# Taking a reciprocal root from GpSimd to ScalarE and VectorE, and splitting an exponential block

## The reference

```python
xn = _layernorm(x)
q, k, v = xn @ Wq.T + bq, xn @ Wk.T + bk, xn @ Wv.T + bv   # 16 heads, 4 key/value heads, width 32
q, k = _rope(_rmsnorm(q, qn_w)), _rope(_rmsnorm(k, kn_w))
# local attention: each token sees itself and 64 tokens before it
local = softmax(where(mask, -10000, q @ k.T * scale)) @ v @ Wo.T + bo
# routed attention: one key and value head is chosen for each token
gating = softmax(xn @ W_gate.T); head = argmax(gating)
k_shared, v_shared = fk[head], fv[head] * max(gating)
routed = causal_softmax(q2 @ k_shared.T / sqrt(32)) @ v_shared
return x + local + routed
```

## Time and profile before

| what | us |
|---|---|
| runs | 684.29, 685.91, 686.01 |
| median | 685.91 |
| span of the profiled execution, first to last instruction | 684.4 |
| TensorE busy | 646.0 |
| VectorE busy | 496.3 |
| GpSimd busy | 442.6 |
| ScalarE busy | 362.5 |

### The profile page before, as it was taken

How to read it: one execution, slowest core, us unless ns; L and a number is a source line. 1 busy time by engine, 2 the same in 40 slices (tenths; PEclk the granted TensorE clock), 3 DMA queues, 4 the chain that set the end, 5 groups by cost and what they waited for, 6 DMA issues and landing times.

```text
span 684.4 us, 19451 instructions
## 1 busy us (share of the span) xinstructions
PE 646.0 (94%) x7432; PEld 510.2 (75%) x7432; DVE 496.3 (73%) x1328; ACT 362.5 (53%) x906; POOL 442.6 (65%) x368
## 2 busy tenths in 40 slices
PE   3788999999999899999899899999999999999997
PEld 3577888887788688888688667777777777777775
DVE  3956966677678866787676368888888787879454
ACT  4436444472527344445335555556566566656674
POOL 3965764938195735684487267685868777778730
PEclk9979999999999999999999999999999999999999
DMA  8522213231232032222214541321314131402011
GB/s 295 206 59 86 82 38 115 86 98 51 66 102 61 30 112 70 64 70 74 77 32 118 158 142 56 96 64 50 111 49 110 51 106 32 110 28 87 4 33 33
DMA packets 64942, 56.61 MB, mean 83 GB/s; under 512 B 6481, under 2 KB 48849, under 8 KB 64849
## 3 DMA queue, kind: packets, MB, share of 16 engines
q1 hardware_dynamic: 62704, 54.45, 27.2%
q10 hardware_dynamic: 2144, 0.93, 0.5%
HBM read 37.20 MB, written 17.89 MB: 80 GB/s over the span
## 4 chain that ended last, share of the span: by engine, by line
PE 78%; DVE 9%; POOL 4%; ACT 3%; issue 2%; DMA 2%; ACTq 1%; DVEq 0%; POOLq 0%
PE gemm L938 17%; PE s_ps L1047 12%; PE od_ps L1096 11%; PE st_ps L1080 10%; PE gemm L1024 6%; PE od_ps L1110 5%; PE win L998 3%; PE gemm L934 3%; PE win L983 2%; PE s_ps L1119 2%; DMA rope_t<-rope 2%; PE av L1010 2%; DVE l_sum L1266 2%; ACT p_loc L1492 2%; DVE l_max L1257 1%
## 5 line engine op out<-in xcount | busy, mean ns | idle before, releaser
L938 PE MATMUL gemm<-w_tok,xt 128*128 128x512 f32 (+1 forms) x768 | 186.1, 384 | 3.3 <-DVE x_res L1283 0.9
L938 PEld LDWEIGHTS gemm<-w_tok,xt 128*128 128x128 f32 x768 | 131.7, 193 | 28.2 <-issue 1.4
L1318 DVE CUSTOM_DVE_ANT_0 s_ps<-s_ps,x_ln 128x512 f32<-128x512 f32 (+3 forms) x224 | 127.6, 620 | 24.4 <-PE s_ps L1047 24.0
L1047 PE MATMUL s_ps<-k_stack,w_tok 96*128 96x512 f32 (+2 forms) x336 | 101.5, 385 | 0.3 <-DVE x_res L1283 0.3
L1080 PE MATMUL st_ps<-w_tok,k_stack 98*128 98x512 f32 x288 | 99.0, 413 | 0.2 <-ACT p_loc L1540 0.2
L1540 ACT ACTIVATE p_loc<-st_ps 128x512 f32<-128x512 f32 x144 | 77.7, 599 | 36.0 <-PE st_ps L1080 34.8
L1634 POOL TENSOR_TENSOR rope_b<-qkv,sin_t 128x128 f32<-128x128 f32 (+1 forms) x32 | 27.5, 880 | 79.5 <-DVE qkv L1232 79.3
L1047 PEld LDWEIGHTS s_ps<-k_stack,w_tok 96*128 96x128 f32 x336 | 55.0, 188 | 28.3 <-DVE picked_fk L1318 12.4
L1492 ACT ACTIVATE p_loc<-win,l_max 128x96 f32<-128x96 f32 x256 | 60.9, 391 | 19.1 <-DVE l_max L1257 19.0
L934 PE MATMUL gemm<-xt,w_qt 128*128 128x256 f32 x384 | 57.1, 293 | 6.3 <-DVE picked_fv L1211 3.5
L1540 ACT ACTIVATE p_loc_t<-st_ps 128x512 f32<-128x512 f32 x96 | 52.4, 599 | 19.8 <-PE st_ps L1080 19.3
(11 more groups left out here) (172 smaller groups left out, 1298.7 us busy)
## 6 DMA issues: line engine op xcount, KB each, us to landing
w_tok<-q_parts SPq DMA_DIRECT2D x72, 128.0 KB, 2.6
q_parts<-qt SPq DMA_DIRECT2D x120, 64.0 KB
x_ln<-x SPq DMA_DIRECT2D x8, 512.0 KB, 4.7
x_res<-x SPq DMA_DIRECT2D x16, 256.0 KB, 2.9
partial<-x_res SPq DMA_DIRECT2D x16, 256.0 KB, 2.6
w_tok<-partial SPq DMA_DIRECT2D x8, 512.0 KB, 5.2
raw<-w_tok SPq DMA_DIRECT2D x3, 1024.0 KB, 12.9
v_win<-v_rows SPq DMA_DIRECT2D x64, 48.0 KB, 2.2
```

The costliest lines, as they stand in the source:

```text
L938: i = e.matmul(g[:, 0:cols], xs[l][:, k, a * P:(a + 1) * P], w_tok_p[r][:, k, c0:c0 + cols], start=first, stop=last)
L1047: e.matmul(s_ps[bank][:, 0:cols], q_op[b][0:HALVES, i, h, :], k_stack[0:HALVES, b * S + c0:b * S + c0 + cols], start=True, stop=True).then ...
L1318: e.tensor_tensor_reduce(out=s[:, 0:cols], in0=s[:, 0:cols], in1=causal[:, S - width + c0:S - width + c0 + cols], scale=1.0, scalar=dst if ...
```

## The change

The power on GpSimd (step 2 above) goes. In its place, ScalarE takes the logarithm of `rms_v` and the exponential of -1/2 times it, into `rms_e` (plan step `q_root`), and VectorE makes one Newton step of three instructions, y = e (1.5 - 0.5 e e v), into `rms_y` (plan step `q_newton`). The table set that holds both functions is loaded once, before the first exponential. Mean + eps is now formed from a tensor of eps, by another kind of instruction. The 16 exponentials of a local tile, one step of the plan before, are four steps of four, between which the plan can put other work of ScalarE. The last two chunks of qt wait in the plan for the last tile's norm, and in `first_maxima` the order of two small steps around a `yield` changes.

```diff
@@ take_q @@
         do("q_rms", n, a)
+        yield 0, [("V", 1.3)]
+        do("q_root", n, a)
+        yield 0, [("A", 0.5)]
+        do("q_newton", n, a)
+        yield 0, [("V", 0.6)]
         do("q_rope", n, a)
-        yield 0, [("V", 1.1), ("G", 3.6), ("G", 1.6), ("", SLACK)]
+        yield 0, [("G", 1.4), ("", SLACK)]
+        p.roped = (n, a) == LAST_TILE
         yield from attend(n, a)

     def take_qt(n, kind, c, freed):
+        while (n, c) in LAST_CHUNKS and not p.roped:
+            yield None
@@ attend @@
-        do("weights", m, a)
-        def exps_end(end):
-            win_free[:] = [end - 1.1 * (HKV - 1 - g) + HOP for g in range(HKV)]
-        yield 0, [("A", 4.4)], exps_end
+        for g in range(HKV):
+            do("weights", m, a, g)
+            yield 0, [("A", 1.1)], lambda end, g=g: win_free.__setitem__(g, end + HOP)
@@ first_maxima @@
         do("max_in_rows", 0, 0)
-        yield 0.11, [("A", 0.27)]
         do("max_low", 0, 0)
-        yield 0, [("V", 0.35)]
+        yield 0.11, [("A", 0.27), ("V", 0.35)]
@@ vector_program @@
-                e.tensor_scalar(rms_v[:, :], rms_t[:, :], 1.0 / DK, RMS_EPS, ALU.mult, ALU.add).then_inc(
-                    *M["rms_v_r"].did((n, a)))
+                e.scalar_tensor_tensor(rms_v[:, :], rms_t[:, :], 1.0 / DK, rms_eps[:, :].to_broadcast([P, NH]),
+                                       ALU.mult, ALU.add).then_inc(*M["rms_v_r"].did((n, a)))
+
+            elif step == "q_newton":
+                n, a = key
+                lane.wait_ge(*M["rms_e"].of((n, a)))
+                e.scalar_tensor_tensor(rms_t[:, :], rms_e[:, :], -0.5, rms_e[:, :], ALU.mult, ALU.mult).then_inc(
+                    *seq.did())
+                lane.wait_ge(*seq.now())
+                e.tensor_tensor(rms_t[:, :], rms_t[:, :], rms_v[:, :], ALU.mult).then_inc(*seq.did())
+                lane.wait_ge(*seq.now())
                 if n or a:
-                    lane.wait_ge(*M["rms_r"].of(tile_before(n, a)))
+                    lane.wait_ge(*M["rope_r"].of(tile_before(n, a)))
+                e.scalar_tensor_tensor(rms_y[:, :], rms_t[:, :], 1.5, rms_e[:, :], ALU.add, ALU.mult).then_inc(
+                    *M["rms_r"].did((n, a)))
@@ scalar_program @@
+        e.preload_act_table_set("natural_log_exp_and_others")
         e.activation(warm[:, :], minus_half[:, :], ACT.Exp).then_inc(*M["warmed"].did())
+            elif step == "q_root":
+                n, a = key
+                lane.wait_ge(*M["rms_v_r"].of((n, a)))
+                if n or a:
+                    lane.wait_ge(*M["rms_r"].of(tile_before(n, a)))
+                e.activation(rms_e[:, :], rms_v[:, :], ACT.Ln).then_inc(*M["rms_l"].did((n, a)))
+                lane.wait_ge(*M["rms_l"].of((n, a)))
+                e.activation(rms_e[:, :], rms_e[:, :], ACT.Exp, scale=-0.5).then_inc(*M["rms_e"].did((n, a)))
@@ gpsimd_program @@
-            elif step == "q_rms":
-                n, a = key
-                lane.wait_ge(*M["rms_v_r"].of((n, a)))
-                if n or a:
-                    lane.wait_ge(*M["rope_r"].of(tile_before(n, a)))
-                e.tensor_tensor(rms_y[:, :], rms_v[:, :], minus_half[:, :].to_broadcast([P, NH]), ALU.pow).then_inc(
-                    *M["rms_r"].did((n, a)))
```

26 lines of the change are left out of this document (15 added, 11 removed).

## The result

The changed kernel takes 726.5 us (725.4 to 726.6) against 686.0 us of the kernel before: a ratio of 1.0588, 95% interval 1.0564 to 1.0612. The forecast was 683.1 us, with 691 us as its upper end. It is wrong in sign and by 43 us. One further execution, in which TensorE's matmuls took longer throughout, took 1122.1 us and is left out.

A forecast was written before the change was run, and what follows sets the result against it. TensorE was taken as nearly full, with 32.8 us not busy in the first stage to win. Terms -1.1 - 1.9 + 1.2 - 1.0 = -2.8 us gave 683.1 us from 685.91; range 678 to 691 for 8 in 10.

The forecast's parts named there:

- Term 1: First tile: norm slightly earlier, three products fill TensorE's wait before the transposes; -1.1 us (bounds 0 and -1.15).
- Term 2: Around 52 to 56 us: exponentials in four steps let a copy and a bank-freeing pick come sooner; -1.9 us (-0.5 to -2.0).
- Term 3: Middle of first stage: 18 us of VectorE stalls cost TensorE 5.8 us, less 4.6 us regained; +1.2 us (-6 to +14).
- against it stands what the same reshuffle gives back: Between 180 and 340 us, 4.6 us of TensorE's 8.1 us hole could close, as exponentials no longer block ScalarE.
- Term 4: End of first stage: last tile's scores start 2.1 us sooner, scaled weights hang on later exponentials; -1.0 us (-3 to +2).
- The power frees VectorE of nothing: Across tiles: GpSimd's power does not hold VectorE up, so removing it gives VectorE 0 us.
- the Newton step stalls VectorE: Rival, middle: Newton instructions wait behind GpSimd's 2.76 us scaling, with a bank's read behind them; 691.7 us, chance 0.21.
- The reshuffle wins more: Rival: earlier norms and split exponentials shrink the 8.1 us hole of 180 to 340 us to 2; 678.1 us, chance 0.15.
- full TensorE hides it all: Rival: the 3.0 us won before 60 us are lost again in the new order's other holes; 685.9 us, chance 0.29.
- No table was reloaded: Judges the rival that logarithm and exponential need other tables, two loads per tile on ScalarE; above 700 us, chance 0.01.
- The routed stage is the same: After the first stage: every engine's list is the same in both kernels from the routed stage's two first scores on.
- What would show it: Forecast's list of profile signs for right or wrong, such as over 3 us idle between 60 and 180 us if wrong.

The follow-up runs named there:

- after_newton_first: Changed kernel with VectorE's Newton step moved ahead of the sum l_sum and its reciprocal in six tiles, other engines' order kept; 715.0 us, ratio 1.0420.
- after_order_exp: Changed kernel without the Newton step, ScalarE's exponential writing rms_y itself, order otherwise the same; 706.5 us, ratio 1.0284.
- after_order_pow: Changed kernel's order, with GpSimd's power in place of the logarithm, exponential and Newton step; 706.7 us, ratio 1.0300.
- The nudges: Kernel before with one assumed planner time changed, same instructions: power 3.6 to 3.4 us, 689.0 us; exponentials 4.4 to 4.2 us, 699.9 us.
- pow_early_block: Changed kernel with GpSimd's power for the new arithmetic and exponentials planned as one block, the plan still assuming an early norm; 734.8 us, ratio 1.0720.

## Why the prediction was wrong, point by point

- **Term 1 (-1.1 us, the first tile): not there.** The transposes no longer wait, as forecast, and rms_y is ready at 37.0 us (forecast 37.3). But the wait did not go, it moved to the three products put ahead of them. Changed kernel, timeline of 37 to 40 us, VectorE and TensorE:

```profile
36.82 0.18 DVE L1263 SCALAR_TENSOR_TENSOR rms_y<-rms_t,rms_e 128x20 f32<-128x20 f32 x1
36.91 0.16 DVE L1192 TENSOR_REDUCE g_rank<-g_score 128x1 f32<-128x16 f32 x1
37.11 1.32 DVE L1194 TENSOR_SCALAR g_hot<-g_score,g_rank 128x16 f32<-128x16 f32 x1
38.35 0.41 DVE L1270 TENSOR_TENSOR qt<-gemm,qt 128x256 fp32r<-128x256 f32 x1
```

```profile
38.82 1.65 PE L944 MATMUL gemm<-w_tok,xt 128*128 128x512 f32 x3 [1.03 <-DVE qt L1270]
```

  The step "TensorE, free from 39.01 - 1.15 = 37.86, is busy with them until 38.7" failed: these products need the bank that qt L1270 frees, and g_hot ahead of it stood 1.32 us behind GpSimd's multiplication (1.26 us from 37.14), which the earlier norm puts there. I had asked when the norm is ready, not when the bank of what fills the hole is free.
- **Term 2 (-1.9 us, the exponentials): half.** The stretch of 52 to 56 us is busy for 3.34 us against 2.01, 1.3 us better. Over the first 60 us the idle time is the same to 0.1 us, so no lead came out of terms 1 and 2.
- **Term 3 (+1.2 us, the middle): this is the step that failed.** Its first half was right: VectorE's stall behind the scaling, forecast as 18 us, measured in the three Newton groups as 10.2 + 7.0 + 5.9 less 16 x (0.178 + 0.115 + 0.178) = 15.6 us. Six tiles, not four, had it behind the scaling. Its price was wrong, in four ways. First, "0.32 us for each us" had been read from the order of before, where the stalls stood beside other work (and it divides the waits of 200 to 340 us by the stalls of 60 to 340). The Newton step puts its stall ahead of bank reads: 19.1 us of time for 15.6 of stall. Of that, the waits are 55.8 - 43.9 = 11.9 us and TensorE's longer busy time is 384.1 - 376.0 = 8.1 us. Second, "against it stands what the same reshuffle gives back", 4.6 us, had the wrong sign: the order alone costs 20.7 us, 11.3 of waits and 9.2 of busy time (from the table: 43.9 - 32.6, 376.0 - 366.8). This part keeps the new form of rms_v, too. Third, the three instructions themselves, 11 us of VectorE in the forecast, had been priced at nothing because VectorE and ScalarE "have more idle than that in the first stage". after_newton_first, where they never stall, is still 8.5 us above after_order_exp, so the 19.1 us are not all the price of stalls. Fourth, the bound of +14 "if TensorE loses 1 us for each" was no bound, since a wait can take the clock with it: 23.2 us of waits brought 17.3 of slower matmuls.
- **Term 4 (-1.0 us, the end of the stage): wrong in sign, small.** In the last 20.8 us TensorE is busy for 15.7, so it stands still for 5.1 us against 4.1, at a clock of 0.84.
- **The power frees VectorE of nothing: right.** after_order_pow and after_order_exp agree within 0.2 us, with intervals of 1.3 and 2.1 us to either side, and VectorE's busy time does not fall without the power. In the profile of before, fk_stack ran seven times within a power, in 0.17 to 0.20 us each. By the rule of the Trainium skill that the prediction weighed (SBUF — State Buffer, Who interferes with whom), it should have been held up.
- **The rival "the Newton step stalls VectorE" had the mechanism and the sign**, with a chance of 0.21 and a price of 691.7 us. It had no term for the clock and none for a worse order. "The reshuffle wins more" was refuted, and so was "full TensorE hides it all". No table was reloaded: the trace has one load, of 1.28 us, at the start.
- **The routed stage is the same: right** (284.1 and 284.2 us).
- "What would show it" named the signs that came: idle time of more than 3 us between 60 and 180 us (8.7), waits on bank reads behind the Newton lines, ScalarE waiting before the logarithm (18.1 us in 7 waits).

Still open: the 14.8 us that the new order costs with the short scaling. The nudges show that orders this close differ by up to 14 us, and pow_early_block that the early norm is worse than that by itself; which of its placements does it was not isolated. The new form of rms_v is in these 14.8 us, too.

## What to carry to other kernels

Where one engine is full and others feed it in order, do not price a new instruction by its own length alone, or by what stalls cost elsewhere in the trace. Ask what stands behind it in its queue, and what long GpSimd instruction can run beside it; cutting that one into four was worth 22 us in the changed kernel and 3 us in the one before. A planned order is part of the kernel: cross order and arithmetic in separate kernels before judging either, and nudge one planner number to see how far an order alone moves the time. Waits of TensorE can be paid twice, when its clock falls behind them, so a bound on a loss must hold both.

## What the runs showed of the hardware that I had not expected

- The clock can fall behind waits that are short against the stage, but does not always: in the changed kernel TensorE stood still for 1.60 and 3.53 us between 148.9 and 155.7 us, and the mean granted clock of 140 to 160 us was 0.88, that of 160 to 180 us 0.95. Behind waits of 1.32 and 2.41 us between 201.6 and 207.0 us it stayed at 1.00. In all, 23.2 us more of waits came with 17.3 us more of busy time for the same matmuls.
- GpSimd's power, 3.5 us on 128x20, does not hold VectorE up (fk_stack ran in 0.17 to 0.20 us within one, seven times) and taking it away gained nothing (706.7 and 706.5 us), while a multiplication of 2.8 us on 128x1536 does. The scaling in four instructions takes 3.21 us instead of 2.79 and is still the better one.
- Of three small VectorE instructions the first two, at 229.56 and 229.71, ran at their shortest around the start of GpSimd's scaling at 229.72, and the third, at 229.92, was held for 2.62 us. So which instruction is caught depends on a few tenths of a us.
